# Moving GpSimd's addition of the input block and b2 from before the scaled input to behind the copy of the small scalars

## What is computed

```python
def delta(x, ...):                       # per sequence, T = 512, C = 256
    q, k, v = split(x @ gates_w + gates_b, 3); lr = x @ lr_w + lr_b
    k = k / norm(k)
    A = tril(k @ k.T, -1) + eye(T)
    u = solve_triangular(A, v, lower=True)
    y = (q @ k.T) @ (lr * u)
    return y @ out_w + out_b
def attn(x):
    x = x + delta(layernorm(x, dn_g, dn_b), ...)
    return x + relu(layernorm(x, mn_g, mn_b) @ w1 + b1) @ w2 + b2
x = x + attn(layernorm(x))
x = x + (silu(n(x) @ wg.T) * (n(x) @ wu.T)) @ wd.T        # n = layernorm; hidden size 768
```

## Time and profile before

| what | value |
|---|---|
| median of 3 runs | 1763.86 us (1761.67 to 1764.37) |
| the profiled execution, its own time | 1764.44 us |
| its span, first to last instruction | 1762.7 us |
| granted TensorE clock, mean share of full speed | 0.982 |
| PE busy in the span | 94% |
| POOL busy | 51% |
| DVE busy | 69% |

### The profile page before, as it was taken

How to read it: one execution, slowest core, us unless ns; L and a number is a source line. 1 busy time by engine, 2 the same in 40 slices (tenths; PEclk the granted TensorE clock), 3 DMA queues, 4 the chain that set the end, 5 groups by cost and what they waited for, 6 DMA issues and landing times.

```text
span 1762.7 us, 31724 instructions
## 1 busy us (share of the span) xinstructions
PE 1661.6 (94%) x11298; PEld 1510.1 (86%) x11298; DVE 1222.9 (69%) x2796; ACT 823.7 (47%) x1754; POOL 895.9 (51%) x1212
## 2 busy tenths in 40 slices
PE   5899999579999999999999999999999999999997
PEld 4899999458888888888888888888888888888886
DVE  4677777237777776777777767777777666666664
ACT  3677777224444444444444444444444444444442
POOL 4456776234555554554444555545545554455551
PEclk8999999789999999999999999999999999999999
DMA  4755565411111121111112311111112111121200
GB/s 116 233 183 190 203 204 201 174 43 44 55 55 55 55 91 55 55 55 55 55 56 64 92 55 55 55 55 55 55 55 79 55 55 55 56 62 63 63 13 25
DMA packets 131700, 145.34 MB, mean 82 GB/s; under 512 B 60885, under 2 KB 113368, under 8 KB 131544
## 3 DMA queue, kind: packets, MB, share of 16 engines
q1 hardware_dynamic: 131544, 143.31, 25.4%
HBM read 82.13 MB, written 61.15 MB: 81 GB/s over the span
## 4 chain that ended last, share of the span: by engine, by line
PE 45%; POOL 19%; issue 8%; DVE 7%; ACT 1%; POOLq 0%; DMA 0%; DVEq 0%; ACTq 0%
PE ps L153 22%; PE ps L1007 14%; POOL xh L1468 5%; POOL xa L1457 4%; POOL xa L1462 4%; PE ps L921 4%; PE ps L938 3%; PE ps L1017 3%; DVE bs L1414 2%; POOL xn L1446 2%; POOL sc L1436 2%; DVE a L1409 2%; DVE wt L1230 1%; POOL sc L1439 1%; PE ps L927 1%
## 5 line engine op out<-in xcount | busy, mean ns | idle before, releaser
L1486 POOL TENSOR_TENSOR hl<-hf,hh 128x512 fp32r<-128x512 f32 x128 | 166.9, 1304 | 401.8 <-ACT hh L1134 401.8
L1017 PE MATMUL ps<-wdT,hh 128*128 128x256 f32 x768 | 204.2, 303 | 0.8 <-ACT sg L1129 0.6
L1017 PE MATMUL ps<-wdT,hl 128*128 128x256 f32 x768 | 187.1, 281 | 2.0 <-DVE hl L1277 2.0
L1134 ACT ACTIVATE hh<-hf 128x512 fp32r<-128x512 f32 x192 | 120.8, 629 | 134.1 <-DVE hf L1272 130.9
L1272 DVE TENSOR_TENSOR hf<-ps,sg 128x512 f32<-128x512 f32 x192 | 132.4, 690 | 66.5 <-PE ps L1007 65.1
L1129 ACT ACTIVATE sg<-ps 128x512 f32<-128x512 f32 x192 | 113.9, 593 | 125.9 <-PE ps L1007 125.7
L1138 ACT ACTIVATE z_hi<-ps 128x256 fp32r<-128x256 f32 x128 | 49.4, 386 | 257.6 <-PE ps L938 257.6
L1007 PE MATMUL ps<-xh3T_hi,wgT 128*128 128x512 f32 x384 | 154.6, 403 | 0.7 <-DVE xh3T_lo L1277 0.7
L1007 PE MATMUL ps<-xh3T_hi,wuT 128*128 128x512 f32 x384 | 152.3, 397 | 0.0
L1007 PE MATMUL ps<-xh3T_lo,wgT 128*128 128x512 f32 x384 | 152.1, 396 | 0.0
L1007 PE MATMUL ps<-xh3T_lo,wuT 128*128 128x512 f32 x384 | 151.9, 396 | 0.0
(11 more groups left out here) (216 smaller groups left out, 5655.7 us busy)
## 6 DMA issues: line engine op xcount, KB each, us to landing
gg_scratch<-gg SPq DMA_DIRECT2D x32, 640.0 KB, 3.3
gg<-gg_scratch SPq DMA_DIRECT2D x32, 640.0 KB, 3.9
kx_scratch<-kx SPq DMA_DIRECT2D x32, 522.0 KB, 2.7
kx<-kx_scratch SPq DMA_DIRECT2D x32, 522.0 KB, 3.6
xk<-in_L_attn_x_dram SPq DMA_DIRECT2D x32, 512.0 KB, 4.2
xt<-in_L_attn_x_dram SPq DMA_DIRECT2D x32, 512.0 KB, 4.7
out_dram<-ot SPq DMA_DIRECT2D x32, 512.0 KB, 2.9
low_scratch<-gg SPq DMA_DIRECT2D x128, 16.0 KB, 1.5
```

What stands on the lines that cost most here:

```text
L1017: mm = pe.matmul(ps[:, (FG, FU)[j // 2], (j % 2) * C:(j % 2 + 1) * C], part[:, h, blk(j)], wdT[:, h, :], start=(h == 0 and part is hh), st ...
L1134: act.activation(hh[:, h, :], hf[:, h % 2, :], ACT.Copy).then_inc(hh_ev[h], 1)
L1486: pool.tensor_tensor(hl[:, h, :], hf[:, h % 2, :], hh[:, h, :].bitcast(F32), ALU.subtract).then_inc(hl_ev[h], 1)
```

## The change

In GpSimd's pass the instruction `xa = xt + b2` is taken from its place in front of `xh` and put behind `shf`. Its wait for `xa_done` goes with it, and so does its signal `xb_done`. Nothing else changes; no instruction is added or dropped.

```diff
                     if att:
                         wait(pool, xin, i * 16)
                         pool.wait_ge(kx_in, (i + 1) * 16)
-                        after(pool, xa_done, i)
-                        pool.tensor_tensor(xa[:, :, :], xt[:, :, :], b2_bc[:, :].unsqueeze(1).broadcast_to([P, TB, C]),
-                                           ALU.add).then_inc(xb_done, 1)
                         for k in range(CB):
                             after(pool, ht_ps[k], i)
                         after(pool, xhm_lo, i)
...
                         for j in range(TB):
                             after(pool, x2_ev[j], i)
                         pool.tensor_tensor(shf[:, :], kx[:, E_SH:E_SH + TB], zero4[:, :], ALU.add).then_inc(sh_done, 1)
+                        after(pool, xa_done, i)
+                        pool.tensor_tensor(xa[:, :, :], xt[:, :, :], b2_bc[:, :].unsqueeze(1).broadcast_to([P, TB, C]),
+                                           ALU.add).then_inc(xb_done, 1)
                     if r == 0:
                         wait(pool, inv_out, 32 * m)
                         invert_start(pool, lanes, m)
```

## The result

The changed kernel takes 1794.14 us (median of 4 runs, 1791.08 to 1796.02) against 1762.76 (4 runs, 1761.41 to 1764.37): a ratio of 1.0176, 95% interval 1.0158 to 1.0194. It is slower. The forecast was 1792.0 us in a range of 1781 to 1804. The profiled execution took 1796.02 us, with a span of 1794.2 us, 31.5 more than before.

A forecast was written before the change was run, and what follows sets the result against it. PE, busy 94% of the span, was taken to set the pace of passes. A loss of 53.3 us less a gain of 25.2 made +28.1 us on 1763.86, so 1792.0 us, range 1781 to 1804.

The forecast's parts named there:

- The bound: Whole pass of 42.85 us: PE, busy 94%, sets the pace; a new PE standstill costs its whole length.
- The gain: PE's L938 of block 2: idle time for `wt` goes, 0.84 us a pass, 30 passes, 25.2 us (at least 17.7).
- The cost at nothing on GpSimd's and SP's queues: Behind `shf`: POOL is idle there, addition ends 5.7 us before `hl`, SP asks for `xb_done` later; cost nothing.
- The holding of `xn`: Block 0: addition holds VectorE's first `xn`, `wt` 1.72 us late a pass, 31 passes, 53.3 us lost (42.8 to 58.6).
- Theory A: Experiments' theory: the loss is VectorE's `xn` held while the addition has SBUF, not the late place; 53.3 us in 31 passes.
- What the duration of `xn` had said: `xn` takes 0.407 us, not 0.27, as if at half rate; this spoke against holding and for a faster kernel.
- the first rival: Block 0: `xn` isn't held, or both are done before the addition; kernel gains 25.2 us, 1738.7 us; chance 0.08.
- The term that was mis-sized: Passes 8 and 16: MEMSET behind the addition may hold the second `xn`; -0.6 to +1.3 us for both, taken as nothing.
- the sum: Whole kernel: loss 53.3 less gain 25.2 makes +28.1 us, median 1792.0 us, 1.6% slower.

The follow-up runs named there:

- e1: Changed kernel, but GpSimd waits for VectorE's four third-norm `xn` instructions before the addition behind `shf`: 1739.19 us, 0.9861 of before.
- e7: Changed kernel, but the addition moved to the end of GpSimd's pass, behind the four `hl`: 1735.24 us, 0.9851 of before.
- e2: Kernel before, with the addition done twice, at its old place and again behind `shf`: 1818.78 us, 1.0309 of before.
- e4: Changed kernel, but the four `xn` of the third norm run on ScalarE instead of VectorE: 1734.54 us, 0.9843 of before.
- e3: Changed kernel, but half of the addition (blocks 0 and 1) back in front of `xh`, the rest behind `shf`: 1756.39 us, 0.9967 of before.
- e6: Changed kernel, with the addition cut into four instructions of one block each: 1767.58 us, 1.0032 of before.
- e5: e1 plus a MEMSET of the whole tile `xa` directly behind `shf`, which only writes: 1743.56 us, 0.990 of before.

## Why the prediction was right

**The bound.** Passes go at PE's pace; a gain or loss counts by PE's idle time. Right: 0.84 us taken away and 1.72 put in make 42.85 - 0.84 + 1.72 = 43.73, and the pass shown takes 43.73. By the medians of the table it is +0.82 and not +0.88. The exact hit owes something to the pass that was chosen: it is one of the shortest of the kernel before, 42.85 us with 0.59 us of idle time at L938, where the median pass takes 42.90.

**The gain.** Forecast 0.84 a pass from pass 1; measured 5.45 - 4.61 = 0.84, and alone, in e1, 0.88 a pass. e1 forecast 1737.6, measured 1739.2.

**The cost at nothing on GpSimd's and SP's queues.** Right: `hl` still waits 7.42 us for ScalarE behind the addition, and e7 shows that even a delayed load of `xt` costs nothing. In the changed kernel SP issues that load at 997.77, 18.6 us behind the addition's end. (That the signal comes "some 15 us later" was a slip: its own rows give 966.70 - 953.73 = 13.0.)

**The holding of `xn`.** Forecast from the MEMSET of pass 16: first `xn` to `wt` 2.86 us, 1.72 more. Measured 976.72 to 979.58, 2.86. The addition started 0.09 behind the first `xn` (forecast 0.08). The lengths of the passes give 43.72 - 42.02 = 1.70 (against e1) and 1.68 (e2). e2 has this cost alone, e4 takes away the one that is held, e1 the one that holds, e3 and e6 change its length. Theory A holds in all five.

**What the duration of `xn` had said.** It spoke for the first rival, and it misled. The Trainium skill (SBUF — State Buffer, "Who interferes with whom") exempts a VectorE instruction with one SBUF input only outside the two-port modes, and says that one with two SBUF inputs contends only with a GpSimd instruction that reads. `xn` has one input, and in e5 a MEMSET, which only writes, holds it in every pass; by the page this is possible only if `xn` runs in a two-port mode. The mode itself isn't in the trace. The same section has it that whoever issues first gets the ports. Here `xn` starts 0.07 to 0.10 us ahead by the profile in every ordinary pass of the changed kernel and of e5 and is the one that is held; the measurement decides. It doesn't show who came first at the ports: the last section has an `xn` with the same lead that wasn't held.

**The term that was mis-sized.** For passes 8 and 16 I had taken nothing, within -0.6 and +1.3 us for both. Pass 16 of the changed kernel (timelines of VectorE and TensorE, then the busy time and granted clock of four stretches, the first pair in pass 16 and the second in pass 8; the columns are length, PE, PEld, DVE, ACT, POOL, PEclk, DMA share, GB/s):

```profile
1064.17 3.85 DVE L1255 TENSOR_SCALAR xn<-x,sc 128x256 f32<-128x256 f32 x2
```

```profile
1068.46 1.22 PE L938 MATMUL ps<-wt,x 128*128 128x256 f32 x2 [2.47 <-DVE wt L1230]
```

```profile
1064.46:1068.46 4.00, 1.53 (x14) 1.32 (x12) 4.00 (x4) 0.00 (x0) 3.33 (x3) 0.94 0.01 2
1068.00:1071.00 3.00, 2.54 (x10) 2.21 (x11) 2.07 (x6) 0.81 (x2) 0.00 (x0) 0.50 0.10 35
713.76:717.76 4.00, 1.52 (x13) 1.31 (x12) 4.00 (x4) 0.00 (x0) 3.34 (x3) 1.00 0.00 0
717.00:721.00 4.00, 3.24 (x23) 2.86 (x24) 3.60 (x9) 1.49 (x4) 0.18 (x1) 1.00 0.24 87
```

The `xn` pair waits for the addition and for the MEMSET behind it, 3.85 us, which makes pass 8 longer than its neighbours by 44.63 - 43.73 = 0.90. In pass 16 the granted clock is 0.50 of full speed (1.2 GHz) from 1068.0 on for some 3 us, and L938 takes 1.22 us instead of 0.70; this pass is 45.84 - 44.63 = 1.21 longer than pass 8. In the kernel before, the two passes took 43.14 and 43.20 us against a median of 42.90. So they cost 0.7 + 1.8 = 2.5 us together, 1.2 above the bound that I had given.

**The total, and what was luck in it.** The span grew by 31.5 us against the 28.1 of the sum. The starts of `gl_lo` in both profiles split this. Passes 2 to 30 have 26.1 us more, where the sum has 29 x 0.88 = 25.5: the ordinary ones are 0.06 us short of the forecast each, which makes 1.7 us, passes 8 and 16 have 2.5 too much, and pass 24 has 0.5 too little (its addition came late; see the last section). Pass 1 has 2.4 more instead of 1.7, and the stretch from the last `gl_lo` to the end 2.6 instead of 0.9; all that comes before pass 1 has 0.3. In pass 1 and near the end the changed kernel has a stretch at half the clock more than the kernel before, which runs at full clock from 394 to 1735 us (busy time and granted clock of the changed kernel, same columns):

```profile
409.20:412.60 3.40, 3.40 (x15) 3.07 (x15) 1.65 (x5) 1.58 (x3) 0.00 (x0) 0.50 0.00 0
1750.60:1754.00 3.40, 3.40 (x15) 3.17 (x14) 1.41 (x3) 0.00 (x0) 0.00 (x0) 0.50 0.00 0
```

That these stretches make the extra 0.7 and 1.7 us isn't shown. So the forecast of 1792.0, 2.1 us below the measured median, is a little closer than its terms were: errors of both signs are in it, the largest of them 2.5 us.

## What to carry to other kernels

Before moving an instruction of GpSimd into idle time of its own queue, look at what VectorE does in that stretch: an instruction that is free on its own engine can hold another engine's for its whole length. The best witness is an instruction of a similar kind that already stands at the place in a few passes; here the MEMSET of two passes gave the price of 1.72 us to 0.04, while the duration of the instruction that would be held pointed the wrong way. If the place is bad, its order need not be given up: a wait for the neighbour's signal (e1), another engine for the neighbour (e4) or a later gap (e7) turned 1.8% slower into 1.4 to 1.6% faster.

## What was unexpected of the hardware

One pass gives the experiment by itself. In pass 24 of the changed kernel GpSimd's `shf` started 0.27 us late without a cause that the profile shows (timelines of GpSimd and VectorE):

```profile
1416.27 0.23 POOL L1476 TENSOR_TENSOR shf<-kx,zero 128x4 f32<-128x4 f32 x1 [0.27 <-issue]
1416.46 2.54 POOL L1478 TENSOR_TENSOR xa<-xt,b_bc 128x1024 f32<-128x1024 f32 x1
```

```profile
1416.04 0.73 DVE L1255 TENSOR_SCALAR xn<-x,sc 128x256 f32<-128x256 f32 x2
...
1417.57 1.91 DVE L1255 TENSOR_SCALAR xn<-x,sc 128x256 f32<-128x256 f32 x2
```

The addition started 0.42 us behind the first `xn` instead of 0.09, and the first pair went through in 0.73 us; of the second pair, the first instruction was held. Passes 12 and 27 of e2 and of e3 repeat this for the first pair, with the same 0.42 us and the same 0.73. The prediction's first rival was to decide at 0.4 us later than taken. Here 0.33 was enough for the first pair, but not for the second, which the rival had left out: it lies behind `wt` and would have met the addition anyway.

The same pass has an `xn` that won. The second one of the first pair starts 0.10 us ahead of the addition, and it is not held:

```profile
1416.36 0.41 DVE L1255 TENSOR_SCALAR xn<-x,sc 128x256 f32<-128x256 f32 x1
```

The addition took 2.54 us there instead of 2.37, as if it were the one that waited. The same lead of 0.1 us in a timeline goes with holding in one case and with none in the other, so it doesn't tell which of the two had been first.

The clock: an idle time of PE of 2.47 us came with half the clock in pass 16, one of 2.48 us in pass 8 did not, and in e2 both passes had it, with 2.49 and 2.48 us. What tells them apart is open. In the 4 us up to the end of the wait PE was busy for 1.53 us in pass 16 of the changed kernel and for 1.52 in pass 8.
